# PE's order in the first seven batches of an attention and expert kernel, and where its 221 rows are cut

## The reference

```python
h = tok(x)                                      # three patch sizes 8, 16, 32 at half overlap: 127 + 63 + 31 = 221 rows of 128
z = layernorm(h)
q, k, v = split(z @ w_qkv)                      # 8 heads of 16
attn = softmax(q @ k.T / sqrt(16))
h = h + (attn @ v) @ w_agg + b_agg
z2 = layernorm(h)
h = h + ffn(z2)                                 # 8 experts, top 2; only rows 0 to 1023 of all 16 * 221 have experts
```

## Time and profile before

| | us |
|---|---|
| median of 3 runs | 269.61 |
| lowest, highest | 268.11, 270.89 |
| the profiled execution | 267.78 |
| its span | 266.0 |

### The profile page before, as it was taken

How to read it: one execution, slowest core, us unless ns; L and a number is a source line. 1 busy time by engine, 2 the same in 40 slices (tenths; PEclk the granted TensorE clock), 3 DMA queues, 4 the chain that set the end, 5 groups by cost and what they waited for, 6 DMA issues and landing times.

```text
span 266.0 us, 7015 instructions
## 1 busy us (share of the span) xinstructions
PE 251.3 (94%) x2759; PEld 206.8 (78%) x2759; DVE 217.1 (82%) x474; ACT 149.4 (56%) x244; POOL 127.9 (48%) x178
## 2 busy tenths in 40 slices
PE   7999989999899999999999999999999999998991
PEld 7799867777576779887777988888888797876771
DVE  3994679879989989788886979798989898888742
ACT  4770332825261525343437978796969696878350
POOL 4000031103348474748575165667676766855422
PEclk9999999999999999999999999999999999999998
DMA  6999300089301010101111103031313122122122
GB/s 210 418 391 464 130 1 0 2 246 316 90 22 27 28 30 28 27 28 27 30 44 38 40 10 54 19 51 29 51 29 53 27 40 34 16 34 19 30 22 44
DMA packets 17151, 21.30 MB, mean 80 GB/s; under 512 B 2392, under 2 KB 12224, under 8 KB 17088
## 3 DMA queue, kind: packets, MB, share of 16 engines
q1 hardware_dynamic: 12400, 17.68, 20.0%
q0 software_dynamic: 4336, 2.60, 7.9%
q10 hardware_dynamic: 384, 0.57, 0.7%
HBM read 16.44 MB, written 5.95 MB: 84 GB/s over the span
## 4 chain that ended last, share of the span: by engine, by line
PE 65%; DVE 24%; POOL 2%; DMA 2%; ACT 2%; issue 2%; SPq 0%; DVEq 0%; POOLq 0%; ACTq 0%
PE e_ps L1194 12%; PE s_ps L1286 10%; PE s_ps L1194 8%; PE m_ps L1400 7%; PE m_ps L1467 5%; DVE nmax L959 4%; PE m_ps L1268 3%; DVE k_b L935 3%; PE m_ps L1258 2%; PE e_ps L1482 2%; PE e_ps L1467 2%; DMA x_raw<-x 2%; DVE x_lo L821 2%; DVE o_tok L985 1%; PE m_ps L1374 1%
## 5 line engine op out<-in xcount | busy, mean ns | idle before, releaser
L959 DVE TENSOR_REDUCE nmax<-s_ps 128x4 fp32r<-128x884 f32 (+1 forms) x60 | 61.7, 1069 | 8.5 <-PE s_ps L1286 8.3
L632 ACT ACTIVATE probs<-s_ps 128x888 f32<-128x888 f32 (+1 forms) x60 | 51.2, 904 | 20.2 <-PE s_ps L1286 20.2
L527 POOL DMA_INDIRECT out<-y_sb,idx_u x23 | 36.9, 1602 | 26.4 <-DMA out<-y_sb,idx_u 23.5
L465 POOL TENSOR_TENSOR var_eps<-mv,eps_t 128x2 f32<-128x2 f32 x16 | 8.5, 531 | 62.7 <-DVE mv L914 62.6
L498 POOL DMA_INDIRECT z_slots<-z,slot_u x20 | 23.4, 1172 | 15.3 <-PE s_ps L1286 11.0
L1400 PE MATMUL m_ps<-probs,v_aug 128*32 128x221 f32 (+1 forms) x480 | 25.8, 353 | 0.0
L1482 PE MATMUL e_ps<-w_now,hidT 128*128 128x128 f32 x184 | 23.2, 276 | 0.0
L1286 PE MATMUL s_ps<-k_a,q_hi 32*128 32x222 f32 (+1 forms) x252 | 19.1, 309 | 3.7 <-DVE q_lo L929 2.2
L1482 PEld LDWEIGHTS e_ps<-w_now,hidT 128*128 128x128 f32 x184 | 22.4, 192 | 0.1
L1286 PEld LDWEIGHTS s_ps<-k_a,q_hi 32*128 32x128 f32 (+1 forms) x252 | 11.9, 169 | 12.5 <-issue 5.7
L693 ACT ACT_TABLE_LOAD x16 | 20.5, 1283 | 0.3
(11 more groups left out here) (181 smaller groups left out, 602.2 us busy)
## 6 DMA issues: line engine op xcount, KB each, us to landing
w_raw<-wt SPq DMA_DIRECT2D x6, 512.0 KB, 9.8
x_raw<-x SPq DMA_DIRECT2D x6, 512.0 KB, 10.9
w_sb<-w SPq DMA_DIRECT2D x1, 2048.0 KB, 9.7
z_slots<-z SPq DMA_DIRECT2D x1, 1518.0 KB, 15.0
zs<-z_slots SPq DMA_DIRECT2D x7, 198.0 KB, 2.5
x_raw<-x SPq DMA_DIRECT2D x4, 256.0 KB, 5.3
out<-h SPq DMA_DIRECT2D x11, 64.0 KB
c_sb<-consts SPq DMA_DIRECT2D x1, 600.0 KB, 13.1
```

The source lines that it names most:

```text
L527: g.indirect_dma_start(rows, bass.IndirectOffsetOnAxis(ap=idx_u[:, at:at + 1], axis=0), y_sb[:, n % 2, i, :], None, compute_op=ALU.add).th ...
L632: s.activation(probs[0:n, blk, 2 * f:2 * f + 2].rearrange("p t u n -> p t (u n)"), s_ps[0:n, 2 * f:2 * f + 2, 0:2 * NE], ACT.Exp, scale=DH ...
L959: v.tensor_reduce(nmax[0:n, blk, 2 * f:2 * f + 2, DH:DH + 2], src, AX_X, ALU.max, negate=True).then_inc(max_ready, 1)
```

## The change

It changes PE's order in the cycles up to 6. z_turn(c+2) is issued at the end of cycle c, and no longer z_turn(c+1) between the halves of the first scores; the p1 taps are issued after s1(c, 1). Up to batch 5 the result of aggregate goes to the upper half of bank 0, beside v, and no more to bank 2; so aggregate waits for q_ready in place of max_in, residual waits for v_done as well, pv waits for h1_ready of the batch before, and z_turn waits for h1_ready from batch 9 on only. The blocks become 104 and 117 rows; that touches slices, tables and the sizes of stores and scatters.

```diff
-N0, N1 = P, N - P
+N0 = 104
+N1 = N - N0
...
+        def agg_bank(b):
+            if b == BATCH - 2:
+                return e_ps[:, 2 * P:4 * P]
+            return m_ps[:, 0, 2 * P:4 * P] if b + 3 < LATE_Z else m_ps[:, 2, 0:2 * P]
...
 def residual(b):
-                src = e_ps[:, 2 * P:4 * P] if b == BATCH - 2 else m_ps[:, 2, 0:2 * P]
-                v.tensor_tensor(dst, src.rearrange(...
+                if b + 3 < LATE_Z:
+                    dve.wait_ge(v_done, b + 3)
+                v.tensor_tensor(dst, agg_bank(b).rearrange(...
...
 def z_turn(b):
-                if b >= 3:
+                if b >= LATE_Z:
                     pe.wait_ge(h1_ready, b - 2)
-                pe.transpose(m_ps[:, 2, 0:N0], z_sb[:, 0, :], ident)
+                pe.transpose(m_ps[:, 2, 0:N0], z_sb[0:N0, 0, :], ident[0:N0, 0:N0])
...
 def pv(b, rs=range(2)):
                 pe.wait_ge(probs_ready, b * 4 + 4)
                 pe.wait_ge(v_ready, b + 2)
+                if b:
+                    pe.wait_ge(h1_ready, b)
...
 def aggregate(b):
                 pe.wait_ge(oT_ready, b + 1)
-                if b + 1 < BATCH - 1:
+                bank = agg_bank(b)
+                if b + 3 < LATE_Z:
+                    pe.wait_ge(q_ready, b + 3)
+                elif b + 1 < BATCH - 1:
                     pe.wait_ge(max_in, b + 2)
-                    bank = m_ps[:, 2, 0:2 * P]
                 else:
...
                 if here:
                     s1(c, 0)
-                if ahead1 and c + 1 < LATE_Z:
-                    z_turn(c + 1)
                 if n > 0:
                     hidden(n, 0)
                 if behind:
                     pv(c - 1)
-                tok_some(p1)
                 if here:
                     s1(c, 1)
+                tok_some(p1)
                 if ahead1 and c + 1 >= LATE_Z:
                     z_turn(c + 1)
...
                 tok_some(p4)
+                if c + 2 < LATE_Z:
+                    z_turn(c + 2)
```

More of the change, by code:

```diff
@@ L46, in ffn_rows @@
 def ffn_rows(b, t):
-    return max(0, min(TILE_N[t], T_FFN - N * b - P * t))
+    return max(0, min(TILE_N[t], T_FFN - N * b - N0 * t))
 FFN_TILES = [(b, t) for b in range(FFN_B) for t in range(2) if ffn_rows(b, t)]
@@ L401, in store_h1k @@
                 sp.wait_ge(h1_ready, b + 1)
-                sp.dma_start(out[b][0:N0, :], h1k[:, b, 0, :]).then_inc(first_stored, 16)
+                sp.dma_start(out[b][0:N0, :], h1k[0:N0, b, 0, :]).then_inc(first_stored, 16)
                 sp.dma_start(out[b][N0:N, :], h1k[0:N1, b, 1, :]).then_inc(first_stored, 16)
@@ L409, in store_h1 @@
                         sp.wait_ge(y_out[i], 16 * sum(ROUND_TILES[i::2]))
-                sp.dma_start(out[b][0:N0, :], h1[:, b % 2, 0, :]).then_inc(stored[b % 2], 16)
+                sp.dma_start(out[b][0:N0, :], h1[0:N0, b % 2, 0, :]).then_inc(stored[b % 2], 16)
                 if b == BATCH - 1:
@@ L1007, in residual @@
                         dve.wait_ge(stored[b % 2], 32 * ((b - FFN_B) // 2))
-                src = e_ps[:, 2 * P:4 * P] if b == BATCH - 2 else m_ps[:, 2, 0:2 * P]
-                v.tensor_tensor(dst, src.rearrange("p (t d) -> p t d", t=2), hb[:, b % 4], ALU.add).then_inc(h1_ready, 1)
+                if b + 3 < LATE_Z:
+                    dve.wait_ge(v_done, b + 3)
+                v.tensor_tensor(dst, agg_bank(b).rearrange("p (t d) -> p t d", t=2), hb[:, b % 4], ALU.add).then_inc(h1_ready, 1)
             def last_pads(b):
@@ L1235, in h_turn @@
                 h = hT[:, b // GROUP, b % GROUP]
-                pe.transpose(m_ps[:, 1, 0:P], h[:, 0:N0], ident)
+                pe.transpose(m_ps[0:N0, 1, 0:P], h[:, 0:N0], ident)
                 pe.transpose(m_ps[0:N1, 1, P:2 * P], h[:, N0:N], ident).then_inc(h_turned, 1)
@@ L1276, in project_v @@
                     pe.wait_ge(q_ready, b + 1)
-                pe.matmul(m_ps[:, 0, 0:P], zT[:, 0:N0], wqkv_sb[:, 4, :], start=True, stop=True)
+                pe.matmul(m_ps[0:N0, 0, 0:P], zT[:, 0:N0], wqkv_sb[:, 4, :], start=True, stop=True)
                 pe.matmul(m_ps[0:N1, 0, P:2 * P], zT[:, N0:N], wqkv_sb[:, 4, :], start=True,
@@ L1285, in four @@
                     rs = slice(32 * t, 32 * t + rows)
-                    mm = pe.matmul(dst[0:n, i, u * NE:(u + 1) * NE], a[rs, u, P * blk:P * blk + n],
+                    mm = pe.matmul(dst[0:n, i, u * NE:(u + 1) * NE], a[rs, u, N0 * blk:N0 * blk + n],
                                    b[rs, u, :], start=start, stop=stop)
@@ L1333, in place_pair @@
                     n = TILE_N[blk]
-                    w = P if blk == 0 else NE - P
-                    mm = pe.matmul(e_ps[64 * f:64 * f + 64, P * blk:P * blk + w],
+                    w = N0 if blk == 0 else NE - N0
+                    mm = pe.matmul(e_ps[64 * f:64 * f + 64, N0 * blk:N0 * blk + w],
                                    nmax[0:n, blk, 2 * f:2 * f + 2].rearrange("p t r -> p (t r)").bitcast(F32),
@@ L1372, in place_max @@
                     n = TILE_N[blk]
-                    w = P if blk == 0 else NE - P
-                    mm = pe.matmul(m_ps[:, 2, P * blk:P * blk + w], nmax[0:n, blk].rearrange("p t r -> p (t r)"),
+                    w = N0 if blk == 0 else NE - N0
+                    mm = pe.matmul(m_ps[:, 2, N0 * blk:N0 * blk + w], nmax[0:n, blk].rearrange("p t r -> p (t r)"),
                                    ident_r[0:n, 0:w], start=True, stop=True)
@@ L1428, in aggregate @@
                     pe.wait_ge(nmaxT_ready, 1)
-                    bank = e_ps[:, 2 * P:4 * P]
-                pe.matmul(bank[:, 0:P], o_T[:, 0:N0], wagg_sb[:], start=True, stop=True)
+                pe.matmul(bank[0:N0, 0:P], o_T[:, 0:N0], wagg_sb[:], start=True, stop=True)
                 pe.matmul(bank[0:N1, P:2 * P], o_T[:, N0:N], wagg_sb[:], start=True, stop=True).then_inc(agg_done, 1)
@@ L1436, in last_aggregate @@
                 pe.wait_ge(probs_ready, 4 * b + 4)
-                pe.matmul(s_ps[:, 0, 0:P], o_T[:, 0:N0], wagg_sb[:], start=True, stop=True).then_inc(agg_done, 1)
+                pe.matmul(s_ps[0:N0, 0, 0:P], o_T[:, 0:N0], wagg_sb[:], start=True, stop=True).then_inc(agg_done, 1)
                 pe.matmul(s_ps[0:N1, 1, 0:P], o_T[:, N0:N], wagg_sb[:], start=True, stop=True).then_inc(agg_done, 1)
@@ L1606, in constants @@
     for b, t in FFN_TILES:
-        token = N * b + P * t + np.arange(P)
+        token = N * b + N0 * t + np.arange(P)
         for k in range(TOP_K):
@@ L1621, in by_table @@
     for b, t in FFN_TILES:
-        n, at = ffn_rows(b, t), N * b + P * t
+        n, at = ffn_rows(b, t), N * b + N0 * t
         out[0:n, table(b, t)] = a[at:at + n]
```

## The result

The changed kernel takes 276.74 us (median of 4 runs, 276.52 to 277.05), the kernel before 268.86 (median of 4): a ratio of 1.0283, 95% interval 1.0218 to 1.0348. That is 7.9 us slower, where +4.3 was forecast, in the forecast's direction. It lies outside the forecast's own range (272 to 276) and inside the whole one (268.5 to 277.5), which reaches that far for rival (a). The execution profiled took 276.52 us with a span of 274.7, 8.7 more than before. What came is the forecast and rival (a) together: TensorE's clock fell to half, in cycle 0 and once more in cycle 2.

What follows compares the result with a forecast made beforehand. PE's program order was taken to bound cycles 0 to 6. Terms of 1.0 (cycles 1, 4, 5, 6), 1.1 (2, 3) and 2.2 us (0) gave +4.3 on 267.78: 272.1 us; own range 272 to 276, whole 268.5 to 277.5.

Steps and rivals of the forecast that it cites:

- rival (a): Cycle 0: PE's idle stretches bring the clock to half, so 18 taps and project_q take twice as long; about +3 us, 277; chance 0.12.
- start of cycle 0: Before cycle 0's first scores: z_turn(1) moves ahead and waits for ln_z(1), so the scores start near 41.05 for 40.35.
- the order: Cycles 0 to 6: the cost of PE's new program order without any clock term, +4.3 us in sum.
- The mechanism: Between score halves: only pv covers DVE's maxima, so PE idles 0.60 us in cycles 1, 4, 5, 6 and 2.24 in cycle 0.
- cycle 3 repeats the pattern of cycle 2: Cycle 3: DVE comes late as in cycle 2, so it gets the same price, +0.55 us.
- the switch between kinds of matmul: At p1 after pv: 0.17 of p1's 0.67 us was read as this switch and counted as saved.
- Rival (b): Cycles 0 to 6: DVE sets the pace and PE's time is elastic; -2.5 us, 267.1; chance 0.18.
- Its bar of 2.24 us: DVE sets the pace if PE's stretch from second half to place_max, p1 included, takes under 2.24 us.
- Rival (c): Only cycle 0 pays; cheaper switches between kinds of matmul make cycles 1 to 6 come out even; +2.2 us, 271.8; chance 0.20.
- Blocks, waits and the late cycles: Blocks of 104 and 117, the new waits, and cycle 7 and later were each taken to cost 0.

## Why the prediction was right, and where it was short

Lengths of cycles, from the start of one cycle's first scores to the next's, and the start of cycle 0, against the kernel before; "clock held" is the changed kernel with products of zeros in cycles 0 and 2, where the order alone is seen:

| | forecast | clock held | changed kernel |
|---|---|---|---|
| start of cycle 0 | +0.70 | +0.87 | +1.11 |
| cycle 0 | +1.50 | +1.16 | +3.41 |
| cycle 1 | +0.24 | +0.10 | +0.10 |
| cycle 2 | +0.55 | +0.34 | +1.98 |
| cycle 3 | +0.55 | +0.32 | +0.33 |
| cycles 4 to 6 | +0.72 | +0.35 | +0.44 |
| sum | +4.26 | +3.14 | +7.37 |

**The mechanism** was right. The second half starts 2.84 us after the first (forecast 2.85), in cycle 2 after 3.93 (3.98), released by DVE's maxima each time, and the idle time was 0.53 to 0.61 us in cycles 1, 4, 5 and 6 and 2.17 in cycle 0 (0.60 and 2.24). DVE gained nothing: it waits for place_max instead. Put back between the halves, p1 takes the whole loss away; its move alone makes 1.25% of the 2.83%, and the rest comes only where z_turn leaves the same place as well. That cycle 3 repeats the pattern of cycle 2 was wrong: before, its halves were 3.56 us apart without a wait for the maxima, now 3.37 with 0.95 us of idle time. It pays about what cycle 2 pays all the same, +0.32 and +0.34.

**The step that failed is rival (a)**, to which I gave 0.12: the sum has no term for the clock, and the clock cost 2.25 us in cycle 0 and 1.64 in cycle 2. The price worked out for (a), about 3 us for 18 taps and project_q at twice their time, was near for cycle 0, though what ran at half clock was the second half and the taps, and not project_q: 1.07 us for 0.61 and 3.99 for 2.21 with the clock held, 2.24 us more together. Left out was that it can come again: the 1.55 us of idle time in cycle 2, which follow from the forecast's own numbers (3.98 less 0.61 and 1.64, so 1.73), brought the clock down too. I wrote that the rows neither show nor exclude a fall, and so had no ground for a chance as low as 0.12. The Trainium skill (TensorE: Matmul & The Clock Gate, HAM oscillation) says that idle gaps bring the clock to half and that each is paid anew; the trace agrees, with 0.50 in two stretches of the changed kernel and in none before its last matmul in the kernel before. The waits in the page's own example are longer than those here, so by the page (a) was open, and not the one to expect, as the prediction has it.

**Luck** has a part in where the time fell. Rival (a)'s 277 was met within 0.3 us, but by terms that cancel: the order was 1.1 us cheaper than forecast and the kernel before 0.75 us faster than the median forecast from (268.86 for 269.61), while the second fall of the clock (1.64 us) and the longer end (1.3 us in the execution profiled) stood in no sum.

**Too dear by a quarter** was the order: 3.14 for 4.26 us. As I read the rows, the switch between kinds of matmul doesn't vanish with p1's move, it moves and gets cheaper: p1 took 0.56 us behind the scores (0.50 taken), but project_q behind taps 0.74 and not 0.85. So from the first scores to place_max cycle 5 lost 0.04 us (6.09 to 6.13) where -0.44 + 0.04 + 0.50 = +0.10 was forecast, and place_max to the next first scores 0.08 for 0.14. In cycle 0 the same shows: place_max 7.55 us after the first scores with the clock held (41.22 to 48.77), forecast 7.82. The start of cycle 0 was the one term too cheap, +0.87 and +1.11 for +0.70; in the changed kernel's execution ln_z(1) itself started 0.31 us later (40.47 for 40.16), and why stays open.

**Rival (b)** fell: DVE's wait for place_max grew, and no cycle got shorter. (Its bar of 2.24 us leaves out the scores of the second half, which the 2.82 us set against it hold. With them it is 2.85, and PE's stretch in cycle 5 took 3.29, 119.31 to 122.60.) **Rival (c)** had a point: with the clock held cycles 1 and 4 to 6 pay 0.10 to 0.14 us each and not 0.24, but cycles 2 and 3 pay. **Blocks, waits and the late cycles** came out at nothing in the medians, as taken.

## What to carry to other kernels

Work that stands between a product and the consumer that must free its banks is cover: before moving it behind the wait, add up what is left of it against the consumer's time. An idle stretch of TensorE of 1.5 to 2.2 us was paid twice here, once as time and once as half clock on what came after, so the price at half clock of what follows such a wait goes into the forecast as a likely term, not as a remote rival. Where the wait can't be covered with work, a few products of zeros kept the clock here and won about 4 of the 7.9 us back.

## What the runs showed of the hardware

Not expected: the clock fell in cycle 2 with a single idle stretch of 1.55 us behind products that had kept PE busy, and in another kernel with the same order in that cycle it did not. Over all executions profiled without zeros in the gap, the clock fell in cycle 0 each of the four times that PE idled 1.98 to 2.17 us before the second half, and in cycle 2 three of the four times that it idled 1.54 or 1.55 us; it didn't fall behind the 1.24 us in cycle 2 of the kernel with p1 moved alone, nor behind 0.95 us in cycle 3. These are single executions, and what decides between them stays open.

Products of zeros can hold the clock: with them in the gap the granted clock stayed at 1.00 in cycle 0 in both executions profiled, where it fell in all four without them. In cycle 2 it stayed in both as well, but there it also stayed once without.
